# A graph network's first node stage: silu and tanh on ScalarE, the tanh's argument on GpSimd, x loaded once and added once

## The reference, cut to what matters

```python
sc_s = s @ sc_ws * a / 8                       # self connection, 96 scalars
sc_v = einsum('nci,cd->ndi', v, sc_wv) * a / sqrt(32)
pre_s = sc_s + o_s                             # o_*: what the edges summed up, times a
pre_v = sc_v + o_v
scalars = silu(pre_s[:, :64])
gates = sigmoid(pre_s[:, 64:96])
gated = gates[:, :, None] * pre_v
x = layernorm(x + concat([scalars, gated]))    # over the 160 features
```

## Time and profile before

| | us |
|---|---|
| median of 3 runs | 2219.08 (2218.88 to 2225.33) |
| the profiled execution: device time | 2213.97 |
| the profiled execution: span of the trace | 2212.2 |
| first node stage, first to last start of add_table | 770.88 to 1156.06 |
| mean granted TensorE clock of the profiled execution | 0.853 |

### The profile page before, as it was taken

The page is one execution under the profiler, slowest core; times in us unless marked ns, Lnnn a source line. Parts: engine busy times, 40 slices in busy tenths (PEclk is TensorE's granted clock), DMA queues, the critical chain, the costliest instruction groups (busy, mean ns, idle before and its releaser), DMA issues.

```text
span 2212.2 us, 47355 instructions
## 1 busy us (share of the span) xinstructions
PE 1427.5 (65%) x10302; PEld 1309.2 (59%) x10302; DVE 1478.8 (67%) x5824; ACT 1079.7 (49%) x3532; POOL 1507.3 (68%) x2020
## 2 busy tenths in 40 slices
PE   2098888888888566666655998888888888100000
PEld 2087777777777366566554987888888888000000
DVE  3087777777777188888883766555565565188886
ACT  1054444444444157767775545444454454066666
POOL 3067888778787456666664677777777776388876
PEclk7599999999999788999987999999999999555555
DMA  9956666666666578888874776676766776599996
GB/s 388 405 109 139 135 139 135 135 136 134 132 137 145 106 215 260 266 263 267 265 238 148 167 170 159 156 154 155 156 153 162 155 161 132 132 330 354 353 356 251
DMA packets 267990, 439.88 MB, mean 199 GB/s; under 512 B 34992, under 2 KB 145264, under 8 KB 264688
## 3 DMA queue, kind: packets, MB, share of 16 engines
q1 hardware_dynamic: 164400, 306.89, 43.2%
q0 software_dynamic: 75264, 67.79, 22.1%
q10 hardware_dynamic: 28224, 64.24, 7.7%
HBM read 235.50 MB, written 203.27 MB: 198 GB/s over the span
## 4 chain that ended last, share of the span: by engine, by line
POOL 28%; DMA 22%; issue 19%; PE 13%; DVE 6%; ACT 5%; SPq 4%; ACTq 1%; POOLq 0%; DVEq 0%
POOL table L459 13%; DMA table<-sums,row_all 9%; DMA tab<-table 7%; POOL xg L442 7%; DMA xg<-x_rows,src_all 3%; POOL half_rstd L495 3%; SPq L348 3%; DVE res L991 3%; ACT y L788 3%; DMA attrT<-in_attrT 3%; DVE stats L1000 2%; PE ps L590 1%; POOL gate L517 1%; PE ps L628 1%; PE ps L576 1%
## 5 line engine op out<-in xcount | busy, mean ns | idle before, releaser
L459 POOL DMA_INDIRECT table<-sums,row_all x392 | 631.3, 1610 | 351.5 <-ACT sums L742 161.8
L788 ACT ACTIVATE y<-res,shift,rstd 128x160 f32<-128x160 f32 x784 | 343.1, 508 | 233.4 <-POOL rstd L498 193.5
L727 ACT COPY msg<-ps 128x192 f32<-128x192 f32 (+1 forms) x196 | 57.4, 293 | 546.1 <-PE ps L609 541.0
L442 POOL DMA_INDIRECT xg<-in_x_rows,src_all x196 | 201.9, 1030 | 59.6 <-issue 58.4
L442 POOL DMA_INDIRECT xg<-x_rows,src_all x196 | 195.6, 998 | 68.2 <-issue 58.8
L934 DVE SCALAR_TENSOR_TENSOR x1g<-ps,a_all,x1g 128x160 f32<-128x160 f32 x392 | 132.5, 379 | 151.5 <-PE ps L629 151.2
L1000 DVE BATCH_NORM_STATS2 stats<-res 128x6 f32<-128x160 f32 x784 | 195.6, 311 | 4.6
L853 DVE TENSOR_TENSOR prod<-hs,ea_all 128x192 f32<-128x192 f32 x196 | 69.9, 357 | 190.2 <-ACT hs L702 187.9
L889 DVE TENSOR_TENSOR pe<-ps,ea_all 128x192 f32<-128x192 f32 x196 | 70.1, 358 | 166.6 <-ACT msg L727 134.0
L495 POOL TENSOR_TENSOR half_rstd<-var,minus_half 128x8 f32<-128x8 f32 x98 | 167.3, 1707 | 14.0
L590 PE MATMUL ps<-weights,midT 128*128 128x128 f32 (+1 forms) x784 | 165.4, 295 | 15.4 <-DVE msg L894 15.0
(11 more groups left out here) (114 smaller groups left out, 4782.0 us busy)
## 6 DMA issues: line engine op xcount, KB each, us to landing
tab<-table SPq DMA_DIRECT2D x98, 384.0 KB, 3.8
table<-zeros SPq DMA_DIRECT2D x24, 1536.0 KB, 37.4
table<-zeros SPq DMA_DIRECT2D x98, 324.0 KB
tab<-table SPq DMA_DIRECT2D x98, 324.0 KB, 5.1
x_rows<-y ACTq DMA_DIRECT2D x98, 320.0 KB, 3.1
x1g<-x_rows SPq DMA_DIRECT2D x98, 320.0 KB
base_rows<-x1g SPq DMA_DIRECT2D x98, 320.0 KB, 2.7
x1g<-base_rows SPq DMA_DIRECT2D x98, 320.0 KB, 4.8
```

The lines of the kernel that those rows point to most:

```text
L442: pool.indirect_dma_start(out=xg[j % RING][:, t, 0:width], out_offset=None, in_=rows, in_offset=bass.IndirectOffsetOnAxis(ap=src_all[:, at ...
L459: pool.indirect_dma_start(out=table[l], out_offset=bass.IndirectOffsetOnAxis(ap=row_all[:, at:at + 1], axis=0), in_=sums[j % 4][:, t, 0:W] ...
L788: last = nc.scalar.activation(y[u][:, t, :], res[u][:, t, :], ACT.Identity, scale=rstd[u][:, t:t + 1], bias=shift[u][:, t:t + 1])
```

## The change

Each part, engine by engine (line numbers of the changed kernel in brackets):

- ScalarE: four Silu of 64 columns with scale a write the gated scalars straight into res; then one Tanh of 128 columns without scale works in place on gate. Before it a wait for GpSimd's argument stands. `store` and `normalise` move from lags 7 and 6 to 8 and 7. Silu waits for the normalise of g - 8, which is the instruction group just ahead of it on ScalarE.
- GpSimd: `tanh_argument(k)` at lag 0 makes gate = t * a/2 for the 32 gates (128 columns), waiting for add_table(k). `scale_gates(k-1)` makes a/2 * tanh + a/2 in two dependent instructions of 128 columns, since a * sigmoid(a t) = a/2 (1 + tanh(a t / 2)). `powers` moves to lag 5 and has two instructions fewer. half_a = a/2 is made once at the start on VectorE.
- VectorE: `gated0` keeps only the vectors; `residual0` is one addition of 640 columns; it now also waits for the silu.
- TensorE: x turned back lands as one row of 160 for each node, so zT is turned in two halves: one matmul more for each group. n0_ps has the same banks in another arrangement.
- SP: xT and zT are one tile, xzT, loaded by one transfer of 320 KB. `load_table` moves from lag 2 to lag 1.
- gate becomes a ring of 4.

```diff
-        gate = two("gate", [P, T, 96])
+        gate = four("gate", [P, T, V])
...
-                    sp.dma_start(xT[u][:, :], A["xT"][bass.ds(m, 1)].rearrange("a k n -> k (a n)")).then_inc(s_nxT[u], 16)
-                    sp.dma_start(zT[u][:, :], A["zT"][bass.ds(m, 1)].rearrange("a k n -> k (a n)")).then_inc(s_nxT[u], 16)
+                    sp.dma_start(xzT[u][:, :], A["xzT"][bass.ds(m, 1)].rearrange("a k n -> k (a n)")).then_inc(s_nxT[u], 32)
...
-                    run_stages(sp, 0, NG, 10, [(0, load_turned), (2, load_table)], RING)
+                    run_stages(sp, 0, NG, 10, [(0, load_turned), (1, load_table)], RING)
...
-                    wait_count(pool, s_y, g - 7)
                     tt(apart[:, :], st[:, :, 1], st[:, :, 4], ALU.subtract)
-                    tt(squares[:, :], st[:, :, 2], st[:, :, 5], ALU.add)
-                    tt(mean2[:, :], st[:, :, 1], st[:, :, 4], ALU.add).then_inc(s_p1, 2)
+                    tt(both[:, :, :], st[:, :, 1:3], st[:, :, 4:6], ALU.add).then_inc(s_p1, 2)
...
-                    tt(shift2[h][:, :], neg_mean2[:, :], half_rstd[:, :], ALU.mult)
-                    ts(rstd2[h][:, :], half_rstd[:, :], 2.0, None, ALU.mult).then_inc(s_shift, 2)
+                    tt(norm2[h][:, :, :], minus_and_two[:, :, :], half_rstd[:, :].unsqueeze(1).to_broadcast([P, 2, 2 * T]),
+                       ALU.mult).then_inc(s_shift, 2)
...
+                def tanh_argument(g, m, u):
+
+                    pool.wait_ge(s_added, g + 1)
+                    half = half_a[:, bass.ds(m, 1), :].rearrange("p g t -> p (g t)").unsqueeze(2).to_broadcast([P, T, V])
+                    nc.gpsimd.tensor_tensor(gate[u][:, :, :], tab[u][:, :, S:96], half, ALU.mult).then_inc(s_arg, 1)
+
                 def scale_gates(g, m, u):
...
                     pool.wait_ge(s_gate, g + 1)
-                    a = a_all[:, bass.ds(m, 1), :].rearrange("p g t -> p (g t)").unsqueeze(2).to_broadcast([P, T, 96])
-                    nc.gpsimd.tensor_tensor(gate[u][:, :, :], gate[u][:, :, :], a, ALU.mult).then_inc(s_scgate, 1)
+                    pool.sem_inc(s_ptick, 1)
+                    nc.gpsimd.tensor_tensor(gate[u][:, :, :], gate[u][:, :, :], half(), ALU.mult).then_inc(s_gplus, 1)
+                    pool.wait_ge(s_gplus, g + 1)
+                    pool.sem_inc(s_ptick, 1)
+                    nc.gpsimd.tensor_tensor(gate[u][:, :, :], gate[u][:, :, :], half(), ALU.add).then_inc(s_scgate, 1)
...
-                    run_stages(pool, 0, NG, 10, [(0, scale_gates), (4, powers)], RING)
+                    run_stages(pool, 0, NG, 10, [(0, tanh_argument), (1, scale_gates), (5, powers)], RING)
...
                     act.wait_ge(s_added, g + 1)
-                    wait_count(act, s_f, g - 1)
+                    wait_count(act, s_y, g - 7)
                     for t in range(T):
                         a = a_all[:, bass.ds(m, 1), t:t + 1].rearrange("p g t -> p (g t)")
-                        last = nc.scalar.activation(gate[u][:, t, :], tab[u][:, t, 0:96], ACT.Sigmoid, scale=a)
-                    last.then_inc(s_gate, 1)
+                        last = nc.scalar.activation(res[u][:, t, 0:S], tab[u][:, t, 0:S], ACT.Silu, scale=a)
+                    last.then_inc(s_silu, 1)
+                    act.wait_ge(s_arg, g + 1)
+                    nc.scalar.activation(gate[u][:, :, :], gate[u][:, :, :], ACT.Tanh).then_inc(s_gate, 1)
...
-                run_stages(act, l * NG, NG, 10, ([(0, gates), (7, store), (6, normalise)] if l == 0 else [(9, store), (8, normalise)]), RING)
+                run_stages(act, l * NG, NG, 10, ([(0, gates), (8, store), (7, normalise)] if l == 0 else [(9, store), (8, normalise)]), RING)
...
-                    tt(res[u][:, :, 0:S], tab[u][:, :, 0:S], gate[u][:, :, 0:S], ALU.mult)
                     tt(planes(res[u][:, :, S:D]), planes(tab[u][:, :, 96:192]),
-                       gate[u][:, :, S:96].unsqueeze(2).to_broadcast([P, T, 3, V]), ALU.mult).then_inc(s_f, 1)
+                       gate[u][:, :, :].unsqueeze(2).to_broadcast([P, T, 3, V]), ALU.mult).then_inc(s_f, 1)
...
-                    tt(res[u][:, :, 0:M], res[u][:, :, 0:M], x0_ps[u], ALU.add)
-                    tt(res[u][:, :, M:D], res[u][:, :, M:D], z0_ps[u], ALU.add).then_inc(s_res, 1)
+                    dve.wait_ge(s_silu, g + 1)
+                    tt(res[u][:, :, :], res[u][:, :, :], x0_ps[u], ALU.add).then_inc(s_res, 1)
```

More of the change, by code:

```diff
@@ L175, in program @@
         junk = sb("junk", [P, 3 * P])
-        xT = four("xT", [M, GROUP])
-        zT = four("zT", [T * V, P])
+        xzT = four("xzT", [P, GROUP + P])
+        xT = [w[0:M, 0:GROUP] for w in xzT]
+        zT = [w[0:T * V, GROUP:GROUP + P] for w in xzT]
         x1g = eight("x1g", [P, T, D])
@@ L188, in program @@
         stats = [stats2[u // 2][:, u % 2, :, :] for u in range(RING)]
[L189 to L194, removed]
+        apart, apart2, var_in, var4, half_rstd = [
+            sb(n, [P, 2 * T]) for n in ("apart", "apart2", "var_in", "var4", "half_rstd")]
+        both = sb("both", [P, 2 * T, 2])
+        minus_and_two = sb("minus_and_two", [P, 2, 2 * T])
+        norm2 = [sb(f"norm{h}", [P, 2, 2 * T]) for h in range(RING // 2)]
+        shift = [norm2[u // 2][:, 0, u % 2 * T:(u % 2 + 1) * T] for u in range(RING)]
+        rstd = [norm2[u // 2][:, 1, u % 2 * T:(u % 2 + 1) * T] for u in range(RING)]
         y = four("y", [P, T, D])
@@ L225, in program @@
         n1_ps = bank(3, 2 * D).rearrange("p (t c) -> p t c", t=2)
-        n0_ps, x0_ps, z0_ps = [b * (RING // 2) for b in (n0_ps, x0_ps, z0_ps)]
+        n0_ps, x0_ps = [b * (RING // 2) for b in (n0_ps, x0_ps)]
         s_w = sem("weights_loaded")
@@ L652, in _ @@
                                                 (2, nodes1b), (5, sum_pair)], RING)
-                def self_connection(o, z, u, w_m, w_z):
-                    for t in range(T):
-                        mm(o[:, t // 2, t % 2, 0:z], xT[u][:, t * P:(t + 1) * P], w_m[:, :], start=True, stop=True)
-                    for b in range(2):
-                        last = mm(o[:, b, :, z:z + V], zT[u][:, :], w_z[:, b * 2 * V:(b + 1) * 2 * V], start=True, stop=True)
-                    last.then_inc(s_np, 1)
                 def nodes0(g, m, u):
@@ L665, in nodes0 @@
                     wait_count(pe, s_added, g - 1)
-                    self_connection(n0_ps[u], 160, u, self_m[0], self_z[0])
+                    o = n0_ps[u]
+                    for t in range(T):
+                        mm(o[:, t, 0:160], xT[u][:, t * P:(t + 1) * P], self_m[0][:, :], start=True, stop=True)
+                    for b in range(2):
+                        last = mm(o[:, 2 * b:2 * b + 2, 160:192], zT[u][:, :], self_z[0][:, b * 2 * V:(b + 1) * 2 * V],
+                                  start=True, stop=True)
+                    last.then_inc(s_np, 1)
                 def turn_back(g, m, u):
@@ L671, in turn_back @@
                     for t in range(T):
-                        turn(x0_ps[u][:, t, :], xT[u][:, t * P:(t + 1) * P], ident[:, :])
-                    turn(z0_ps[u].rearrange("p t c -> p (t c)"), zT[u][:, :], ident[:, :]).then_inc(s_xb, 1)
+                        turn(x0_ps[u][:, t, 0:M], xT[u][:, t * P:(t + 1) * P], ident[:, :])
+                    for b in range(2):
+                        q = slice(b * 2 * V, (b + 1) * 2 * V)
+                        last = turn(x0_ps[u][:, 2 * b:2 * b + 2, M:D], zT[u][q, :], ident[q, q])
+                    last.then_inc(s_xb, 1)
                 if l == 0:
```

29 lines of the change are left out of this document (19 added, 10 removed).

## The result

The changed kernel took 2211.19 us (median of 20 runs) against 2218.43 for the kernel before (20 runs); the ratio is 0.9963, 95% interval 0.9949 to 0.9977: 7.2 us less by the medians, some 8 by the ratio. A few executions of a kernel, whichever it is, run in a state that takes longer, and all ratios with an interval leave these out. The forecast was 2218, with 2192 to 2248 around it, and chances of 0.33 for "within 0.3%", 0.30 for faster and 0.37 for slower. The time lies in the range, on the faster side just past 0.3%.

What follows compares the result with a forecast made beforehand. Loops of waits, not a full engine, were taken to bound the kernel. Stage +0.7, table load -1.3 and shorter powers -0.7 summed to -1.3 us: 2218 against the median of 2219.08, range 2192 to 2248 (8 in 10).

Steps and rivals of the forecast that it cites:

- The third loop: First node stage, argument, scaling, gated0, add_table, back to argument: 8.10 us a pair of groups, 4.05 a group, against 7.94.
- The dependent gap: Between scale_gates' two instructions on GpSimd, the second needing the first's result: taken as 0.10 us.
- The meeting of powers with gated0: GpSimd's powers running beside VectorE's gated0 in every pair, a small instruction taking 0.52 us instead of 0.20: +0.32.
- The sign given for it: In the changed first node stage, the successor of L485 in powers was to take near 0.5 us in most pairs.
- The slower rival: GpSimd-VectorE loop longer, 128-column instructions at 0.46 us, gaps 0.15: 8.79 us a pair, +31 us, 2249; chance 0.37.
- Its bound of 0.50: Upper figure in us for a 128-column GpSimd instruction, if half the difference were a cost of the shape's four rows.
- the table wait: VectorE waiting 42 times, 28.4 us in 280, for the table before add_table; it was to go with load_table at lag 1.
- loop 1: Kernel before, first node stage: powers, normalise, sigmoids and scaling between GpSimd and ScalarE, 7.77 us a pair; the change opens it.
- the 1.3 us forecast: ScalarE's table load at L708, 1.28 us on the chain, no longer left in or after the stage: -1.3 us.
- the term for powers: Shorter powers on GpSimd at both ends of node stages: -0.7 us.
- the faster rival: GpSimd's new instructions cheap and undisturbed, 0.29 us each: 7.40 us a pair, 2186, half of it 2202 likelier; chance 0.30.

Runs made afterwards that it cites:

- add_table first: The changed kernel with add_table ahead of gated0 in VectorE's list, nothing else: 2150.56 us against 2223.30, ratio 0.9672; once more on another chip 0.9666.
- the added lag: The changed kernel with add_table ahead, gated0 and residual0 at lag 3, bn_stats 4, turning back 2, load_table 0: 2171.52 us against 2222.21, ratio 0.9739.

## Why the prediction held, and where it did not

**The third loop** was the core of the forecast, and it was right in place and size. Forecast 4.05 us a group and 385.9 us for the stage; measured 4.07 and 386.7. The starts were to alternate near 3.0 and 5.1 us, and did at 3.10 and 5.04; each of the two waits, 2 us on VectorE and 1.7 on GpSimd, came once a pair. Undoing it alone (add_table first) took 63 us off the stage, where 62 to 72 had been expected.

**The parts of its sum.** Groups of instructions from 840 to 1120 us (busy, mean ns, idle before):

```profile
L533 POOL TENSOR_TENSOR gate<-gate,half_a 128x128 f32<-128x128 f32 x69 | 27.6, 400 | 0.0
L524 POOL TENSOR_TENSOR gate<-tab,half_a 128x128 f32<-128x128 f32 x69 | 27.5, 399 | 58.7 <-DVE tab L978 58.7
L536 POOL TENSOR_TENSOR gate<-gate,half_a 128x128 f32<-128x128 f32 x69 | 27.5, 398 | 12.4 <-POOL gate L533 12.4
...
L496 POOL TENSOR_TENSOR apart<-apart 128x8 f32<-128x8 f32 x34 | 11.8, 348 | 2.7
L494 POOL TENSOR_TENSOR both<-stats 128x16 f32<-128x16 f32 x34 | 10.0, 295 | 0.0
```

The 128-column instructions: 0.40 forecast on the line between 8 and 384 columns, 0.40 measured. The dependent gap: 0.10 forecast, 0.18 measured. But an instruction of 128 columns that has nothing left to wait for starts 0.36 us after the one before it, not 0.40, so the gates of an iteration take 1.29 us up to the start of powers, for 1.30 forecast. The meeting of powers with gated0: 0.32 forecast; measured L496 0.15 and L494 0.08 above their undisturbed 0.20 and 0.22, 0.23 in all. The sign given for it, the first instruction of powers near 0.5, did not appear: L493 took 0.21, and the meeting fell on the two behind it. Powers with its meeting took 3.79 us, for 3.80 forecast. So the place of the loop was insight, and its length to 0.05 us in 8.15 was in part luck, small misses of opposite sign. VectorE's residual of 640 columns from start to start: 0.72 forecast, 0.73 measured (924.44 to 925.17).

The rivals on either side fall: GpSimd's instructions were neither cheap nor dear. The slower rival, with 0.37 the likeliest of the three cases, leaned on a row overhead and on a figure that no run here shows; the runs show 0.40 us for 128 columns. Its bound of 0.50 was also worked out wrong: half of the 0.63 us as a fixed cost gives 0.20 + 0.32 + 0.10 = 0.62. Nothing in the sum used it.

**The table, x, TensorE, ScalarE.** That the table wait goes and that nothing comes of it was right, as was nothing for the single transfer. The account of the kernel before was incomplete: loop 1 alone costs 8.25 us a pair and not 7.77, as the kernel before with an earlier table showed. No table load stood in the stage, as the built list had it, and the one at the head of the edges of layer 1 is gone. That it gave the 1.3 us forecast is not shown: from the last add_table to the first table_row1 the changed kernel took 772.9 us, before 773.0.

**The step that failed** is the term for powers, "Shorter powers at both ends of node stages: -0.7". The edit of powers alone, shorter and without its wait for y, gave a ratio of 0.9973, which is 3 to 9 us, and the forecast never gave the dropped wait a price. At the end of the program the traces show 1.2 us of it. The rest cannot be placed: the first node stage was no shorter, and the last one varies by 6 us between profiles whatever its powers. With -0.7 for this term the sum was -1.3; the ratio says -5 to -11 for the whole change. Had the term been the 6 us of the run alone, the sum would have been near -7. So the range was kept and the loop was right, but the gain itself was not forecast; that the time fell just past 0.3% on the faster side has nothing to do with the faster rival, cheap instructions on GpSimd.

**The larger miss of insight** is that the prediction named the loop and stopped at its price. The edit that opens it, VectorE's two list entries exchanged, can be read off the same paragraph.

## What to carry to other kernels

When engines run fixed lists in iterations, write down for each new wait which instruction of the waited-for engine stands ahead of the one that is wanted: here add_table stood behind gated0, which wanted the result of the engine that waited for add_table, and exchanging two list entries was worth eight times the change itself. A wait that disappears is worth only the distance to the next loop, and a loop read off one quiet pair may be longer once the wait that kept two engines apart is gone. A lag added to a step also lengthens the life of every buffer that it reads. And before a few microseconds in one stage of one pair of profiles are given a cause, look at the same stage in every other profile whose code is the same there.

## What the runs showed of the hardware

- A GpSimd instruction that waits for the one just ahead of it on GpSimd starts 0.18 us after that one's end (L536, 69 times in 280 us), where gaps of 0.07 to 0.15 had been read in powers.
- GpSimd and VectorE hold each other up when VectorE's instruction reads two SBUF operands: 8 columns on GpSimd took up to 0.80 us instead of 0.20 beside L962 and L963, and with only the lags changed VectorE's 256 columns took 0.69 us in the mean instead of 0.42. The Trainium skill names this contention (GPSIMD Engine Reference, section 1, SBUF interfaces); the traces agree. Beside additions with one operand in PSUM none was seen: L524 at 924.70 beside L992 stayed at 0.40, L496 at 926.78 beside L978 at 0.20, and all 34 lengthened instructions of GpSimd between 840 and 1120 us of the changed kernel ran beside gated0 (L984).
- A stage whose code is the same does not take the same time in each profile: the last node stage took 264.6 us in the changed kernel, 269.1 with add_table first and 270.5 with the added lag. In the same 220 us, a share of the transfers of 0.99 went with 351 GB/s and 1.00 with 359, so the share told that the queues were occupied, not at what rate.
